# Attention a: tile flags summed by their own operation and fetched by ScalarE, maxima sent without a sign change, two row copies moved to ScalarE, two sums of picks merged

## The reference, cut to what matters

```python
topk = max(1, int(Tx * 0.3))                       # 76
scores = jnp.einsum('bhid,bhjd->bhij', q, k) * scale
topk_scores, indices = jax.lax.top_k(scores, topk)
masked = jnp.full_like(scores, -jnp.inf)
masked = masked.at[bi, hi, ti, indices].set(topk_scores)
attn = jax.nn.softmax(masked, axis=-1)
out = jnp.einsum('bhij,bhjd->bhid', attn, v)
return out @ W_out.T + b_out
```

## Time and profile before

| what | us |
|---|---|
| median of three runs | 5300.36 |
| the profiled execution | 5302.46 |
| its span | 5300.7 |
| attention a in it | 95 to about 2541 |
| PE busy in the span | 4709.3 (89%) |
| DVE busy | 4089.0 (77%) |
| ACT busy | 3157.1 (60%) |
| POOL busy | 2522.7 (48%) |

### The profile page before, as it was taken

The page is one execution under the profiler, slowest core; times in us unless marked ns, Lnnn a source line. Parts: engine busy times, 40 slices in busy tenths (PEclk is TensorE's granted clock), DMA queues, the critical chain, the costliest instruction groups (busy, mean ns, idle before and its releaser), DMA issues. The chain is left out here.

```text
span 5300.7 us, 121671 instructions
## 1 busy us (share of the span) xinstructions
PE 4709.3 (89%) x34686; PEld 3284.1 (62%) x34686; DVE 4089.0 (77%) x14487; ACT 3157.1 (60%) x10145; POOL 2522.7 (48%) x3026
## 2 busy tenths in 40 slices
PE   4588888889878898898899999899999998999998
PEld 3344444445444454454688888766666666888887
DVE  3899999999989999999588888655555555888886
ACT  3688888888867888887222222376777775222222
POOL 1466666666656666666544444311111111444444
PEclk6566666666656666656899999999999999999999
DMA  2000000000000000000234443200000001444444
GB/s 70 10 14 10 13 10 13 10 13 10 13 10 10 13 10 13 13 10 10 49 81 84 89 84 80 53 10 10 10 10 10 11 11 36 81 80 82 89 85 96
DMA packets 358589, 188.51 MB, mean 36 GB/s; under 512 B 190691, under 2 KB 346886, under 8 KB 358150
## 3 DMA queue, kind: packets, MB, share of 16 engines
q1 hardware_dynamic: 358150, 183.55, 17.3%
HBM read 147.04 MB, written 11.01 MB: 30 GB/s over the span
## 5 line engine op out<-in xcount | busy, mean ns | idle before, releaser
L844 ACT ACTIVATE junk<-SS,nt 128x256 bf16<-128x256 f32 x3072 | 1516.4, 501 | 207.1 <-POOL nt L482 156.5
L494 POOL TENSOR_SCALAR gone<-SS,mid 128x256 bf16<-128x256 f32 x1024 | 1181.9, 1171 | 759.8 <-DVEq L1038 576.5
L1205 POOL TENSOR_TENSOR f_hid<-f_g_m,f_cbs 128x256 f32<-128x256 f32 x1024 | 745.7, 728 | 849.0 <-DVE f_g_m L1450 622.5
L1305 ACT ACTIVATE f_th<-bank 128x256 f32<-128x256 f32 x1088 | 418.5, 385 | 1146.0 <-PE bank L1236 1146.0
L1235 PE MATMUL bank<-f_xTf,wgT 128*128 128x256 f32 x2176 | 692.6, 400 | 52.1 <-DVE f_g_m L1450 36.4
L1851 DVE TENSOR_REDUCE nmxb<-bank 128x2 f32<-128x512 f32 x512 | 329.2, 685 | 476.1 <-PE bank L1623 476.0
L1236 PE MATMUL bank<-f_xTf,wuT 128*128 128x256 f32 x2176 | 651.8, 381 | 0.0
L644 PE MATMUL bank<-k,q 32*128 32x256 f32 x2048 | 452.7, 574 | 220.0 <-DVE SS L960 216.6
L1267 PEld LDWEIGHTS bank<-wdT,f_hid 128*128 128x128 f32 x4096 | 601.0, 191 | 68.0 <-POOL f_hid L1205 13.2
L1267 PE MATMUL bank<-wdT,f_hid 128*128 128x128 f32 x4096 | 629.7, 276 | 11.0 <-POOL f_hid L1205 10.9
L844 ACT ACTIVATION_READ_ACCUMULATOR junk<-SS,nt 128x1 f32 x3072 | 594.0, 193 | 0.0
(11 more groups left out here) (233 smaller groups left out, 8037.1 us busy)
## 6 DMA issues: line engine op xcount, KB each, us to landing
f_cbs<-f_shares SPq DMA_DIRECT2D x512, 256.0 KB, 5.8
q4x<-q SPq DMA_DIRECT2D x64, 256.0 KB, 2.4
k4x<-k SPq DMA_DIRECT2D x64, 128.0 KB, 2.1
qrow<-q_rows SPq DMA_DIRECT2D x512, 8.0 KB
q_rows<-qTb SPq DMA_DIRECT2D x32, 128.0 KB, 1.7
out_dram<-xres SPq DMA_DIRECT2D x4, 1024.0 KB, 9.3
q4x<-nmx_rows SPq DMA_DIRECT2D x128, 4.0 KB
f_shares<-f_combT SPq DMA_DIRECT2D x64, 32.0 KB, 1.4
```

The source lines that it names most:

```text
L494: last = pool.tensor_scalar(gone[:, h % 4, i, :], SS[:, (u - lag) % 4, c, :], mid[:, (u - lag) % 4, c:c + 1], 0.0, ALU.subtract, ALU.min)
L844: nc.scalar.activation(junk[:, c % 2, :], SS[:, uu % 4, c, :], ACT.Sign, bias=bias(c), accum_out=acc[:, k, uu % 4, c:c + 1]).then_inc(s["s ...
L1205: pool.tensor_tensor(hid[:, e % NBUF, :], g_m[:, e % NBUF, :], cbs[:, par, e, :], ALU.mult).then_inc(s["hid"], 1)
```

## The change

Five things are changed, all in attention a.

- `nmx` and the operation that negates the maxima are gone. SP waits for the last copy of scores itself and sends `mxs`, the maxima as they are; the spare rows of k hold minus one (`minusrow`) instead of one, with one more small operation in the setup.
- The last operation of `picks` writes `fail` as "fine equals 0" and, by its accumulator output, the sum over the 16 columns into a 17th column. PE's `judged` sums 17 columns. The maximum over `flags` (L1036) is gone; the branch looks at the 17th number.
- The copy of the sums into `flags` is made by ACT, at its place h = 4 behind two exponentials. DVE's sequencer waits for it.
- `take_k` and `take_qr` are made by ACT, at h = 7 of even steps and h = 2 of odd steps.
- The two sums `mid` and `nxt` over the picks are one operation over twice as many elements, written into `mid`, which has room for both.

The core of the diff:

```diff
-                nc.vector.tensor_reduce(onerow[:, :], ident[:, :].rearrange("p (n w) -> p n w", w=PAD16)[:, :, HD], AX, ALU.add)
+                own.link(nc.vector.tensor_reduce(minusrow[:, :], ident[:, :].rearrange("p (n w) -> p n w", w=PAD16)[:, :, HD], AX, ALU.add))
+                nc.vector.tensor_scalar(minusrow[:, :], minusrow[:, :], -1.0, None, ALU.mult)
...
-                    wait(sp, s["nmx"], t + 1)
+                    wait(sp, s["evac"], GT * t + GT)
...
-                    sp.dma_start(nmx_rows, nmx[:, u, :]).then_inc(s["copied"], 16)
+                    sp.dma_start(max_rows, mxs[:, u, :]).then_inc(s["copied"], 16)
...
-                        nc.tensor.matmul(M1[0:1, 0:GT], ones128[:, :], fail[:, :], start=True, stop=True).then_inc(s["m1"], 1)
+                        nc.tensor.matmul(M1[0:1, 0:GT + 1], ones128[:, :], fail[:, :], start=True, stop=True).then_inc(s["m1"], 1)
...
+                def take_k(n):
+                    wait(act, s["m1"], n + 1)
+                    nc.scalar.copy(ktok[:, :, :].rearrange("p i d -> p (i d)"), M1[:, 0:T]).then_inc(s["m1c"], 1)
+
+                def take_qr(n):
+                    wait(act, s["m0"], n + 1)
+                    nc.scalar.copy(qtok[:, :, :].rearrange("p i d -> p (i d)"), M0[:, 0:T]).then_inc(s["m0c"], 1)
...
+                        if h == 4 and runs(t, 2):
+                            f1 = m1_before(bb, "f0" if even else "f1")
+                            wait(act, s["m1"], f1 + 1)
+                            nc.scalar.copy(flags[:, :], M1[0:1, 0:GT + 1]).then_inc(s["m1c"], 1)
...
+                            if h == 7:
+                                take_k(m1_before(bb, "ktok"))
...
+                        if not even and front and h == 2:
+                            take_qr(m0_before(bb, "qtok"))
...
-                        if h == 7:
-                            wait(dve, s["evac"], GT * (t + 1) + GT)
-                            V.tensor_scalar(nmx[:, (u + 1) % 4, :], mxs[:, (u + 1) % 4, :], -1.0, None, ALU.mult).then_inc(s["nmx"], 1)
...
-                        mids = own.mark(V.tensor_reduce(mid[:, z2, :], pick[:, 0, :, :], AX, ALU.add))
-                        nexts = own.mark(V.tensor_reduce(nxt[:, :], pick[:, 1, :, :], AX, ALU.add))
+                        both = own.mark(V.tensor_reduce(mid[:, z2, :, :].rearrange("p a t -> p (a t)"),
+                                                        pick[:, :, :, :].rearrange("p a t j -> p (a t) j"), AX, ALU.add))
...
-                        V.tensor_scalar(fail[:, :], fine[:, z2, :], -1.0, 1.0, ALU.mult, ALU.add).then_inc(s["failed"], 1)
+                        V.tensor_scalar(fail[:, 0:GT], fine[:, z2, :], 0.0, 0.0, ALU.is_equal, ALU.add, accum_out=fail[:, GT:GT + 1]).then_inc(s["failed"], 1)
...
                         n1 = m1_before(bb, "f0" if even else "f1")
-                        wait(dve, s["m1"], n1 + 1)
-                        V.tensor_copy(flags[:, 0:GT], M1[0:1, 0:GT]).then_inc(s["m1c"], 1)
                         wait(dve, s["m1c"], n1 + 1)
-                        own.link(V.tensor_reduce(flags[:, GT:GT + 1], flags[:, 0:GT], AX, ALU.max))
+                        dve.sem_inc(s["gate"], 1)
                         redo(dve, V, z2)
```

More of the change, by code:

```diff
@@ L348, in build @@
         nxt = ab("nxt", [P, GT])
[L349 removed]
+        mid = ab("mid", [P, NB4, 2, GT])
         fine = ab("fine", [P, NB4, GT])
[L351 removed]
+        fail = ab("fail", [P, GT + 1])
         flags = ab("flags", [1, GT + 1], mybir.dt.int32)
@@ L360, in build @@
         s = sems("a", "mv rstd xn m0 m0c m1 m1c var sig scores evac signs u0 u1 u2 thr failed flag okay "
-                      "nmx copied turned spgate out pused pt pv on own aown pown slow oc gate pgate upper vput ini inid")
-        nmx_rows = nc.dram_tensor("nmx_rows", (P, GT), f32, kind="Internal").ap()
+                      "copied turned spgate out pused pt pv on own aown pown slow oc gate pgate upper vput ini inid")
+        max_rows = nc.dram_tensor("max_rows", (P, GT), f32, kind="Internal").ap()
         COPIED, TURNED = 48, 32
@@ L493, in outsiders @@
                                 c = 2 * h + i
-                                last = pool.tensor_scalar(gone[:, h % 4, i, :], SS[:, (u - lag) % 4, c, :], mid[:, (u - lag) % 4, c:c + 1], 0.0,
+                                last = pool.tensor_scalar(gone[:, h % 4, i, :], SS[:, (u - lag) % 4, c, :], mid[:, (u - lag) % 4, 0, c:c + 1], 0.0,
                                                           ALU.subtract, ALU.min)
@@ L548, in step @@
                     sp.sem_inc(s["spgate"], 1)
-                    rows = nmx_rows.rearrange("q (e g i) -> e g i q", e=2, i=HALVES)
+                    rows = max_rows.rearrange("q (e g i) -> e g i q", e=2, i=HALVES)
                     for e in range(2):
@@ L801, in take_q @@
                     if m == 2:
-                        last = nc.scalar.activation(k4[:, par, :, :].rearrange("p c t -> p (c t)"), M0[:, :], ACT.Identity, bias=onerow[:, 0:1])
+                        last = nc.scalar.activation(k4[:, par, :, :].rearrange("p c t -> p (c t)"), M0[:, :], ACT.Identity, bias=minusrow[:, 0:1])
                     else:
@@ L820, in _ @@
                 take_qn(4)
+                take_k(0)
+                take_qr(5)
                 take_v(0, 7)
@@ L910, in normed @@
                     n.then_inc(s["xn"], 1)
[L912 to L918, removed]
                 def take_g(n):
@@ L1003, in picks @@
                         own.need(second)
-                        mids = own.mark(V.tensor_reduce(mid[:, z2, :], pick[:, 0, :, :], AX, ALU.add))
-                        nexts = own.mark(V.tensor_reduce(nxt[:, :], pick[:, 1, :, :], AX, ALU.add))
+                        both = own.mark(V.tensor_reduce(mid[:, z2, :, :].rearrange("p a t -> p (a t)"),
+                                                        pick[:, :, :, :].rearrange("p a t j -> p (a t) j"), AX, ALU.add))
                         yield
-                        own.need(nexts)
-                        apart = own.mark(V.tensor_tensor(nxt[:, :], nxt[:, :], mid[:, z2, :], ALU.is_lt))
+                        own.need(both)
+                        apart = own.mark(V.tensor_tensor(nxt[:, :], mid[:, z2, 1, :], mid[:, z2, 0, :], ALU.is_lt))
                         yield
                         own.need(apart)
-                        positive = own.mark(V.scalar_tensor_tensor(tmp[:, :], mid[:, z2, :], 1.0e-6, nxt[:, :], ALU.is_gt, ALU.mult))
+                        positive = own.mark(V.scalar_tensor_tensor(tmp[:, :], mid[:, z2, 0, :], 1.0e-6, nxt[:, :], ALU.is_gt, ALU.mult))
                         yield
@@ L1057, in step @@
                             check_flags()
-                        if front and even and h == 7:
-                            take_k(m1_before(bb, "ktok"))
                         if front and not even:
@@ L1086, in redo @@
                     slow = Own(dve, s["slow"])
-                    any_failed = dve.value_load(flags[0:1, GT:GT + 1], min_val=0, max_val=P)
+                    any_failed = dve.value_load(flags[0:1, GT:GT + 1], min_val=0, max_val=P * GT)
                     with dve.If(any_failed > 0):
```

9 lines of the change are left out of this document (2 added, 7 removed).

## The result

| | before | after |
|---|---|---|
| median of four runs, us | 5300.69 | 5267.38 |
| from, to | 5296.66, 5303.83 | 5265.15, 5273.04 |
| the profiled execution | 5302.46 | 5265.15 |

The ratio is 0.9937 with an interval of 0.9925 to 0.9949: 33 us faster, where 54 were forecast. The time lies inside the range given.

A forecast was written before the change was run, and what follows sets the result against it. DVE, 91% busy in attention a, was taken to set the pace. Terms 13 + 10.5 + 4.3 - 1.2 + 16 + 14.7 - 3 = 54 us gave 5246 us; range 5225 to 5280 us for 8 in 10.

The forecast's parts named there:

- stop at the flag: DVE standing while its sequencer loads the flag and branches; about a second of idle per 1000 us was not claimed, 18.7 us was.
- wait for `upper`: POOL has no slack in odd steps, so DVE hands back about 0.2 us once in four tiles: 3 us lost.
- the flags' two: DVE's two operations on the flags, 0.36 us in even steps, leave DVE.
- I take half, 0.15 us, because the load waits for another engine's semaphore first: Even steps: loading and branching begin up to 0.3 us earlier, under the last copy of scores; half was counted.
- The rival with the sequencer fully ahead: Flag load and branch run fully ahead: even steps give 0.9 us, 28 us instead of 16; about 5231 us, chance 0.11.
- the first kind: 11 of 31 odd steps, where DVE's copy waits and starts 0.24 us behind the sums' start; 0.15 us won each.
- the later kinds of odd step: Odd steps with DVE's copy about 0.5 us (9) or at least 1.0 us (11) behind the sums; 0.42 and 0.84 us won.
- the rival on PE's pace: PE takes the pace in attention a; odd steps keep 0.15 us and half the rest goes: 5274 us, chance 0.14.
- It fits, with 0.2 us left.: Odd steps: after ACT's stop for the sums, counts and oT end at 1206.6, before POOL wants c2 at about 1206.8.
- a sign of being wrong: POOL's shift operation of the second move waiting for ACT's counts in odd steps would show the prediction wrong.
- The slower rival: ACT's new stop in odd steps delays c2, then POOL, kk and DVE; 3 us late gives 5333 us, chance 0.07.
- S: Theory of the follow-ups, not the forecast: ACT's stop at the flags passes through oT and its bank to PE and scores.

The follow-up runs named there:

- less work on PE: Changed kernel without the matmuls that add the bias to v and to the output of attention a: 5266.77 us, ratio 0.9929 to the kernel before.
- `oT` first: Changed kernel, but in odd steps ACT copies oT before the flags: 5261.59 us, ratio 0.9926 to the kernel before.
- DVE fetches in odd steps: Changed kernel, but in odd steps DVE copies the 17 sums of flags itself: 5255.87 us, ratio 0.9919 to the kernel before.
- early ones: Changed kernel, but PE sums the flags before the weighing matmuls and transposes of d = 1: 5232.91 us, ratio 0.9861 to the kernel before.

## Why the prediction was right, and where it was not

Right are the sign, the range, and that DVE set the pace: its own work shrank by what was priced, within 0.1 us. That the time came out inside the range is in part luck. The prediction put DVE's added wait for scores at nothing and it was 45 us; the stops at the flag gave 22 us more than forecast and hid half of that. The 54 us against 38.9 in the stage come out by DVE's ledger:

| DVE in attention a | forecast | measured |
|---|---|---|
| its own instructions and the gaps among them | -59.3 | -59.4 |
| stop at the flag | +2.0 | -20.4 |
| wait for scores | 0 | +44.8 |
| wait for `upper` | +3 | +3.7 |
| the rest | 0 | -7.6 |
| sum | -54 | -38.9 |

*Its own instructions.* The terms priced by distance between starts, 0.21 us for the negation, 0.34 and 0.33 for the copies, 0.36 for the flags' two, 0.07 for the merge and 0.02 back for the accumulator, make 59.3 us over all tiles. The trace has 51.7 us of busy time less and 7.7 us less of the small gaps that no wait is named for. The sum of 480 elements took 646 ns where 650 were worked out. From the start of the first sum to the next free-standing instruction (L922, now L932) DVE took 0.63 us before,

```profile
190.02 0.40 DVE L1004 TENSOR_REDUCE mid<-pick 128x16 f32<-128x240 f32 x1
190.34 0.39 DVE L1005 TENSOR_REDUCE nxt<-pick 128x16 f32<-128x240 f32 x1
190.65 0.28 DVE L922 TENSOR_TENSOR gram<-bank,mask_bd 128x128 f32<-128x128 f32 x1
```

and 0.57 us after:

```profile
187.54 0.65 DVE L1009 TENSOR_REDUCE mid<-pick 128x32 f32<-128x480 f32 x1
188.11 0.28 DVE L932 TENSOR_TENSOR gram<-bank,mask_bd 128x128 f32<-128x128 f32 x1
```

So 0.06 us were saved and 0.07 forecast. The Trainium skill ("VectorE: DVE Perf Modes", the TRN2 errata) states its 151 cycles for an fp32 `tensor_tensor`; taken for this reduction, as an estimate, they would have saved 0.157 us, and the trace does not agree.

*Stop at the flag, even steps.* The step that failed was "I take half, 0.15 us, because the load waits for another engine's semaphore first". The semaphore was raised in time, and in the step shown the whole load and most of the rest ran under the copies of scores. The stops of 28 even steps went from 32.3 to 11.9 us, 20 us gained besides the two operations where I had 5. Part of the mis-sizing lies in the row: the 1.00 us of the earlier trace rows holds in half of the even steps, and the others had 1.30. The odd steps lost 7 us, and the first and last steps gained 7, which makes the 20.4 of the ledger. The rival with the sequencer fully ahead had the right place, and its 0.9 us a step was still too little: a step gained 0.36 and 0.73 us. That ACT has copied the even sums by then held in 12 of the 28 steps only. The Trainium skill ("Advanced Engine Details and Errata", Engine Queue Depths) gives VectorE a queue of 8 instructions; by it the full lead was to be expected, and the trace agrees in kind: the load at 1073.7 us runs before the copy of scores that stands ahead of it has started (1073.95).

*Stop at the flag, odd steps.* 0.49 us from the start of the sums to the load had been worked out. The load starts at 1035.9 against sums at 1035.39, so that came out. The sort starts 1.80 us behind the start of the sums (1037.19 against 1035.39). In a step of the first kind it was 1.90 us where the stop was 1.30 and 1.60 where it was 1.00, so 0.1 us was gained in some and 0.2 lost in others; forecast were 0.15. In all, the stops of 29 odd steps went from 34.6 us to 41.6, 7.0 us longer, where the step's numbers, less what its instructions give, made them 6.7 us longer. That the later kinds of odd step would turn into the first, as the rival on PE's pace had it, can be seen: in 27 of the 29 the sort starts 1.77 to 1.83 us behind the sums, where it was 1.59 to 3.72.

*Wait for scores.* This is the error that counts, a term of 45 us that was put at nothing. Its step is ACT's stop: "It fits, with 0.2 us left." The stop was foreseen at about 2 us (it is 1.67), and its 5.7 us of counts and `oT` were laid beside two of those that wait for ACT, POOL's second move and the next exponentials. A third one waits for the end of that very stretch: PE, for the bank that `oT` is copied out of. It stands in the sum of 5.7 us by name (behind eleven counts, while the kernel has it behind six), and I did not ask who waits for it. Before, PE came to L619 about when the copy was done, with 0.4 us of waits in all; there was no room for 1.67 us. POOL's side did not hold either (the waits of its shift operation for ACT's counts went from 86.7 us in 31 times to 176.8 in 70, between 95 and 2500 us; in odd steps the prediction had named them as a sign of being wrong), but it reached DVE only with the 3.7 us of `upper`, 4 times.

*The slower rival* had the right place, ACT's stop, and the wrong road: it went by POOL and `kk`, not by PE. *The rival of PE's pace* gave 5274 us, nearer to 5267 than the forecast. Its sign that PE's waits for DVE fall under 30 us in 1000 did not come: they are 50.1 there, from 77.9. With the stop in place less work on PE took 11 us from the 45. So its number was near for the most part for another reason.

*How far S reaches.* Taking ACT's stop out of the changed kernel lowered the median by 6 us (`oT` first) and 11.5 us (DVE fetches in odd steps), of the 21 between 5267 and the forecast 5246. The stop is shown as one cause of the missing gain, and not as all of it.

What stays open: why maxima and copies alone bring 25 and 31 us, and why they do not add. A body of the loop, from one pause of DVE at its edge to the next, lasts 148.7 us in the median before (bodies with a refused tile left out). With the maxima alone, the copies alone, all but the flags, and everything it lasts 147.0, 146.5, 146.8 and 146.8 us, though DVE is busy 2201, 2196, 2190 and 2168 us in the stage and only the last has ACT's stop. So in most bodies the changed kernel is hardly faster than the one with the maxima alone; I have not found what holds them there, and no run tests it. The ledger itself is read from one execution of each kernel.

## What to carry to other kernels

When an in-order engine gets a new wait, list every one of its next results in order, up to where its slack swallows the stop, and for each who waits: readers of the data, and writers of the bank that it frees. Move the producer ahead of its long neighbours first, then hand the result to another engine; here the same fetch was worth some 7 us with late sums and some 41 with early ones. And put no other wait ahead of it: the copy of `oT` before the flags, which did no harm with late sums, cost 24 us with early ones. Then read the stop of every step, not of one: here it came in two sizes before and in three after.

## What the runs showed of the hardware

A register load and a branch that stand behind DVE's copies of scores, with their semaphore already raised, leave 0.28 us of DVE's time. Behind an instruction that they depend on they leave 1.00 or 1.30 us. The load itself takes the same, 307 ns in the median before and 304 after:

```profile
L1086 DVEq TENSOR_LOAD <-flags x64: 302/304/552, 166.5 to 2499.1; - x64
```

ACT fetches 17 sums out of PSUM in 163 ns:

```profile
L870 ACT CAST flags<-bank x64: 147/163/164, 164.2 to 2498.8; 1x17 int32<-1x17 f32 x64
```

The granted clock in attention a was 0.63 of the full one before and 0.65 after, and PE was busy 54 us less for the same matmuls. So PE's own work did not grow in the changed kernel; what the clock's changes do to the length of a body was not tested.
